# A four-layer graph network on one core: softmax passes with their weights in PSUM, sums placed by register and one wide addition, and query rows kept in fp32

## The reference

```
x += (segment_sum(h[src]) / (deg + eps)) @ W0.T + b0                        # sum
x += relu(mean over edges of relu([h[src], h[dst]] @ W_edge.T) @ Wn.T + bn)  # mlp
x += GAT(elu(GAT(h)))                                                        # gat, twice
x += attention(h) + h @ Wskip + bskip                                        # dot
```

## Time and profile before

| what | us |
| --- | --- |
| median of 3 runs | 5275.26 (5270.87 to 5277.76) |
| profiled execution | 5274.91 |
| its span | 5273.2 |
| busy PE, PE weight loads | 3318.3 (63%), 2774.7 (53%) |
| busy DVE | 2957.9 (56%) |
| busy ACT | 1684.9 (32%) |
| busy POOL | 3467.1 (66%) |

### The profile page before, as it was taken

One profiled execution on the slowest core, in us unless ns is written; L12 is line 12 of the kernel. 1 busy time (PEld: TensorE's weight loads), 2 busy tenths in 40 slices (PEclk: granted clock), 3 DMA queues, 4 the chain that ended last, 5 costly groups with the idle time before them and its releaser, 6 DMA issues. The chain is left out here.

```text
span 5273.2 us, 118399 instructions
## 1 busy us (share of the span) xinstructions
PE 3318.3 (63%) x30932; PEld 2774.7 (53%) x30933; DVE 2957.9 (56%) x8646; ACT 1684.9 (32%) x5942; POOL 3467.1 (66%) x3551
## 2 busy tenths in 40 slices
PE   1555555667777775666666646666666466666664
PEld 0444444456666563555555535555555355555554
DVE  3222222432222225777777767777777867777777
ACT  2222222332222225444444444444444411111111
POOL 1777777457777772777777537777775076666663
PEclk9666666666666667666666656666666767777776
DMA  4333333233333332444334224433442244444442
GB/s 123 105 106 107 104 104 104 70 100 104 106 106 104 104 87 72 111 109 115 110 109 112 81 73 112 112 109 109 113 110 76 69 144 137 135 139 136 140 135 82
DMA packets 331653, 564.80 MB, mean 107 GB/s; under 512 B 79101, under 2 KB 149773, under 8 KB 331438
## 3 DMA queue, kind: packets, MB, share of 16 engines
q0 software_dynamic: 124288, 289.37, 20.6%
q1 hardware_dynamic: 207170, 273.48, 16.7%
HBM read 490.38 MB, written 72.84 MB: 107 GB/s over the span
## 5 line engine op out<-in xcount | busy, mean ns | idle before, releaser
L1003 POOL DMA_INDIRECT GT<-table,srcI x3520 | 3452.8, 981 | 1687.3 <-issue 1044.2
L1316 PE MATMUL psA<-V,O 128*128 128x144 f32 (+1 forms) x4224 | 970.3, 414 | 45.3 <-DVE acc L1427 40.1
L1316 PEld LDWEIGHTS psA<-V,O 128*128 128x128 f32 x4224 | 901.6, 305 | 108.5 <-DVE acc L1427 75.3
L1427 DVE TENSOR_TENSOR acc<-acc,psA 128x144 f32 (+1 forms) x2112 | 624.7, 296 | 274.3 <-DVE acc L1427 7.6
L1044 DVE TENSOR_TENSOR acc<-acc,psA 128x1032 f32 (+1 forms) x176 | 214.7, 1220 | 685.9 <-PE psA L1123 673.0
L1168 DVE TENSOR_TENSOR prod<-psD,GT 128x1024 f32<-128x1024 f32 x88 | 107.7, 1224 | 679.5 <-DMA GT<-table,srcI 679.5
L1307 PE MATMUL psS<-newM,Ot 128*128 128x16 bf16 (+1 forms) x6336 | 213.2, 175 | 432.9 <-DVE newM L1394 432.9
L1035 PE MATMUL psA<-zerob 1*128 1x258 bf16 (+1 forms) x704 | 179.0, 405 | 484.8 <-issue 453.4
L1307 PEld LDWEIGHTS psS<-newM,Ot 128*128 128x128 bf16 x6336 | 189.6, 102 | 488.5 <-DVE newM L1394 488.5
L1250 ACT COPY nodeM<-newM 128x16 f32 x1408 | 307.8, 219 | 348.0 <-ACT nodeM L1250 226.3
L1181 PE MATMUL psD<-nodeQ,Ot 128*128 x2112 | 283.9, 264 | 130.8 <-DVE prod L1168 125.3
(11 more groups left out here) (217 smaller groups left out, 4965.8 us busy)
## 6 DMA issues: line engine op xcount, KB each, us to landing
Ob<-onehots SPq DMA_DIRECT2D x352, 256.0 KB
Ot<-onehots_turned SPq DMA_DIRECT2D x352, 256.0 KB
GT<-table,srcI POOLq DMA_INDIRECT x3520
onehots<-Ob SPq DMA_DIRECT2D x88, 256.0 KB
onehots_turned<-Ot SPq DMA_DIRECT2D x88, 256.0 KB
first<-first_dram SPq DMA_DIRECT2D x176, 64.0 KB
first_dram<-GT SPq DMA_DIRECT2D x18, 384.0 KB, 5.2
table<-GT SPq DMA_DIRECT2D x40, 144.0 KB, 1.9
```

What stands on the lines that cost most here:

```text
L1003: eng.indirect_dma_start(out=GT[:, p.k, j, 0:table.shape[1]], out_offset=None, in_=table, in_offset=bass.IndirectOffsetOnAxis(ap=srcI[:, p ...
L1316: ins = eng.matmul(psA[:, j, 0:VW], O[:, p.q, j, :], V[:, p.q, j, 0:VW], start=True, stop=True)
L1427: eng.tensor_tensor(a, a, psA[:, j, 0:VW], ALU.add).then_inc(added.sem, 1)
```

## The change

1. Softmax passes, weights: `act_weight` takes the exponential twice, first into PSUM (`factors`, in the fourth bank of `psA`) and then into `V` as before. `dve_values` multiplies by `factors` and so has one input in SBUF and one in PSUM.
2. Softmax passes, sums: the eight tiles of a group are summed into nine places of `psA` by block, three places in each of three banks, where a register gives the offset (`blk_off`, a new table made at the start by six DVE operations). Several tiles of one block accumulate in one place. `act_empty` on ACT writes zeros into the nine places first, once the addition of the group before is done. `dve_add` scales and then adds all nine places to nine consecutive blocks at once; it loads one block number instead of eight.
3. Order: PE does `pe_sums` of group p-2 right behind `pe_maxima` of group p. DVE's `dve_segmax` stands behind the addition. The logits of the target nodes go to the edges two turns ahead in gat too, and `act_stage` three.
4. Query rows (dot) and the target part in mlp: `nodeQ` is kept in fp32; ACT casts `Ot` to fp32 (`turn_32`), and PE does eight fp32 matmuls instead of 24 bf16 ones. The splitting into parts goes from `sum_to_mlp` and `gat_to_dot`. SP's load of `Ot` waits for the cast (`turned32`) instead of the matmuls, in dot beside `maxedge`.

The core of the diff:

```diff
+    PLACES, STRIDE, BANK = 9, 170, 512
...
-        nodeQ = sb("nodeQ", [P, NB, 3, D], BF16)
+        nodeQ = sb("nodeQ", [P, NB, D])
...
+        Ot32 = sb("Ot32", [P, 2, G, P])
...
-                            part_rest(eng, n, n.R[:, :, D:2 * D], kept)
-                            part_2(eng, n, D, nodeQ)
...
-                            eng.copy(n.R, n.ps).then_inc(kept.sem, 1)
-                            part_0(eng, n, n.R[:, :, D:2 * D], nodeQ, kept)
-                            part_1(eng, n, D, nodeQ)
+                            eng.copy(n.R[:, :, 0:D], n.ps[:, :, 0:D]).then_inc(kept.sem, 1)
+                            eng.copy(n.at(nodeQ), n.ps[:, :, D:2 * D]).then_inc(noted_rows.sem, 1)
...
-                            eng.scalar_tensor_tensor(out=n.Y2, in0=n.ps[:, :, 0:D], scalar=Q_SCALE, in1=bias_row(6),
+                            eng.scalar_tensor_tensor(out=n.at(nodeQ), in0=n.ps[:, :, 0:D], scalar=Q_SCALE, in1=bias_row(6),
...
+        def turn_32(eng, p):
+
+            eng.wait_ge(*ring_hotT[p.k](p.i))
+            eng.wait_ge(*toedge(p.g - 2))
+            eng.copy(Ot32[:, p.q, :, :], Ot[:, p.k, :, :]).then_inc(turned32.sem, 1)
+
+        def rows_to_edges(eng, p, b):
+
+            eng.wait_ge(*turned32(p.g))
+            eng.wait_ge(*prodded(p.g - 1))
+            for j in range(G):
+                ins = eng.matmul(psD[:, j, :], Ot32[:, p.q, j, :], at_block(nodeQ, b[j], D), start=True, stop=True)
+            ins.then_inc(toedge.sem, 1)
+
...
+            factors = flatA[:, 3 * BANK:3 * BANK + HG].rearrange("p (g h) -> p g h", g=G)
+            places = flatA[:, 0:3 * BANK].rearrange("p (m e) -> p m e", e=BANK)[:, :, 0:3 * STRIDE]\
+                .rearrange("p m (n w) -> p m n w", w=STRIDE)[:, :, :, 0:VW]
...
+            def act_empty(eng, p):
+
+                eng.wait_ge(*added(p.g - 1))
+                apart(eng)
+                eng.copy(places, consts[:, 0:1, :].unsqueeze(1).to_broadcast([P, 3, 3, VW])).then_inc(emptied.sem, 1)
+
             def act_weight(eng, p):
+
                 eng.wait_ge(*bound(p.g))
+                eng.wait_ge(*values(p.g - 1))
+                eng.activation(factors, by_head(below[:, p.q, 0:HG]), ACT.Exp).then_inc(factor.sem, 1)
                 eng.wait_ge(*sums(p.g - 2))
                 v = V[:, p.q, :, 0:VW].rearrange("p g (h c) -> p g h c", h=h)
                 eng.activation(v[:, :, :, C:C + 1], by_head(below[:, p.q, 0:HG]).unsqueeze(3), ACT.Exp).then_inc(weight.sem, 1)
...
+            def pe_places(eng, p):
+                return loaded(eng, "places", blk_off, p.g, G, 2 * BANK + STRIDE)
+
+            def pe_sums(eng, p, off):
                 eng.wait_ge(*values(p.g))
+                eng.wait_ge(*weight(p.g))
                 eng.wait_ge(*onehot32(p.g))
+                eng.wait_ge(*emptied(p.g))
+                apart(eng)
                 for j in range(G):
-                    if j % 2 == 0:
-                        eng.wait_ge(*added(p.g - 1, j + 1))
-                    ins = eng.matmul(psA[:, j, 0:VW], O[:, p.q, j, :], V[:, p.q, j, 0:VW], start=True, stop=True)
+                    ins = eng.matmul(flatA[:, bass.ds(off[j], VW)], O[:, p.q, j, :], V[:, p.q, j, 0:VW], start=False,
+                                     stop=j == G - 1, skip_group_check=True)
                 ins.then_inc(sums.sem, 1)
...
             def dve_values(eng, p):
-                eng.wait_ge(*weight(p.g))
+                eng.wait_ge(*factor(p.g))
+                eng.wait_ge(*sums(p.g - 2))
                 v = V[:, p.q, :, 0:VW].rearrange("p g (h c) -> p g h c", h=h)
-                eng.tensor_tensor(v[:, :, :, 0:C], heads(GT[:, p.k, :, f0:f0 + D], h),
-                                  v[:, :, :, C:C + 1].to_broadcast([P, G, h, C]), ALU.mult).then_inc(values.sem, 1)
-
-            def dve_scale(eng, p):
-
-                b = loaded(eng, "blocks", blk, p.g, G, NB - 1)
+                eng.tensor_tensor(v[:, :, :, 0:C], heads(GT[:, p.k, :, f0:f0 + D], h), wide(factors, C), ALU.mult)\
+                   .then_inc(values.sem, 1)
+
+            def dve_add(eng, p):
+
+                b = loaded(eng, "block", blk, p.g, 1, NB - 1, G)
                 a = at_block(acc, b[0], VW).rearrange("p (h c) -> p h c", h=h)
                 eng.wait_ge(*rescale(p.g))
                 eng.wait_ge(*added(p.g - 1))
                 eng.tensor_tensor(a, a, wide(resc[:, p.q, 0:h], C + 1), ALU.mult).then_inc(scaled.sem, 1)
-                return b
-
-            def dve_add(eng, p, b):
-
                 eng.wait_ge(*sums(p.g))
                 eng.wait_ge(*scaled(p.g))
-                for j in range(G):
-                    a = at_block(acc, b[j], VW)
-                    if j:
-                        eng.wait_ge(*added(p.g, j - 1))
-                    eng.tensor_tensor(a, a, psA[:, j, 0:VW], ALU.add).then_inc(added.sem, 1)
+                to = acc[:, bass.ds(b[0], PLACES), 0:VW].rearrange("p (m n) w -> p m n w", n=3)
+                eng.tensor_tensor(to, to, places, ALU.add).then_inc(added.sem, 1)
...
+                        if not gat and p.has(2):
+                            turn_32(eng, p.plus(2))
+                        if gat and p.has(3):
+                            act_stage(eng, p.plus(3))
+                        if p.has(1):
+                            act_flags(eng, p.plus(1))
                         if p.has(0):
                             act_rescale(eng, p)
-                        if gat and p.has(2):
-                            act_stage(eng, p.plus(2))
-                        if p.has(1):
-                            act_flags(eng, p.plus(1))
+                        if p.has(-1):
+                            act_empty(eng, p.plus(-1))
                         if p.has(0):
                             act_weight(eng, p)
                             if gat:
                                 act_note(eng, p)
                             act_onehot32(eng, p)
-                    sweep(eng, NG, turn, early=RING)
+                    sweep(eng, NG, turn, early=RING, late=1)
                 @block.tensor
                 def _(eng):
                     def turn(p):
+                        if p.has(-2):
+                            off = pe_places(eng, p.plus(-2))
                         if p.has(0):
                             pe_maxima(eng, p)
-                        if gat and p.has(1):
-                            pe_toedge(eng, p.plus(1))
+                        if p.has(-2):
+                            pe_sums(eng, p.plus(-2), off)
                         if p.has(1):
                             pe_logitT(eng, p.plus(1))
                         if p.has(0):
                             pe_maxedge(eng, p)
                         if p.has(1):
                             pe_segT(eng, p.plus(1))
-                        if not gat and p.has(2):
+                        if p.has(2):
                             pe_toedge(eng, p.plus(2))
-                        if p.has(-1):
-                            pe_sums(eng, p.plus(-1))
-                    sweep(eng, NG, turn, early=2, late=1)
+                    sweep(eng, NG, turn, early=2, late=2)
...
-                            b = dve_scale(eng, p.plus(-2))
+                            dve_add(eng, p.plus(-2))
                         if p.has(1):
                             dve_segmax(eng, p.plus(1))
-                        if p.has(-2):
-                            dve_add(eng, p.plus(-2), b)
                         if p.has(0):
```

79 lines of the change are left out of this document (34 added, 45 removed).

## The result

The changed kernel takes 5177.84 us (median of 4 runs, 5173.40 to 5181.22), the kernel before 5275.75 (4 runs, 5270.87 to 5277.76): a ratio of 0.9815, 95% interval 0.9802 to 0.9827. Forecast were 5171 and 5100 to 5235. The profiled execution took 5178.65, its span is 5176.9, 96.3 us less than before.

The account below looks back on a forecast made before the run. POOL's gathers were taken to bound the gat passes, a cycle through DVE and PE the dot pass. 5274.9 - 110 (gat) - 10 (sum_to_mlp) - 13.4 (gat_to_dot) + 30 (dot) = 5171.5, say 5171 us, range 5100 to 5235.

Parts of the forecast that it names:

- case A: Whole kernel: the terms come out as summed, 5171 us, own range 5140 to 5205; chance 0.50.
- the remainder of contention: Gat passes: short DVE operations with two SBUF inputs still hold POOL 0.05 us a turn (bounds 0 and 0.25).
- The whole difference is this one gather: Gat turn: a 1.62 us gather beside DVE's multiplication explains 10.66 against mlp's 9.98; PSUM weights save 110 us over both passes.
- Dot pass: Dot: the cycle closes through PE at 11.77 us a turn, +30 us for the pass (bounds -51 and +82).
- The 3.84 from product to new maxima: Dot turn: first term of the cycle, 3.84 us from DVE's product to the end of the maxima chain.
- fp32 rows: Dot turn: eight fp32 matmuls replace 24 bf16 ones, 3.6 us (bounds 3.2 and 3.8) instead of 3.21.
- sum_to_mlp: Node phase limited by ACT: two copies of 0.40 us each, 0.6 less a unit, 10 us taken (bounds 5 and 12).
- gat_to_dot: Node phase limited by DVE: two operations of 0.33 us each go, 0.67 x 20 = 13.4 us saved.
- B: Dot turn closes sooner, 10.9 to 11.3 us, -14 to -49 instead of +30: 5092 to 5127 us; chance 0.18.
- C: Gat passes: POOL's long gather stays, the 110 us are gone, 5281 us; chance 0.09.
- D: Gat turn ends at 10.2 to 10.5 us by ACT or PE's cycle: 63 instead of 110, 5218 us; chance 0.16.
- E: Gat passes: zeroing in front of ACT's exponential delays DVE's multiplication; with dot at its upper bound 5376 us, slower; chance 0.07.

Follow-up runs that it names:

- g1_psum_weights: The kernel before with only the gat weights moved to PSUM: 5264.75 us against 5273.37, ratio 0.9982.
- g3_scan_first: The changed kernel with DVE's scan in front of the wide addition in the dot pass: 5016.04 us against 5273.23 for the kernel before, ratio 0.9515.
- g7_bf16_rows: The changed kernel without its fourth part, query rows in three bf16 parts again: 5204.55 us against 5273.37 for the kernel before, ratio 0.9871.
- h9_three_passes: The changed kernel plus SBUF weights (gat 1), 1.05 us more ACT work (gat 2), query rows before the transpose (dot): 6842.33 us against the kernel before's 6945.72.
- f3_scan_first: The changed kernel with DVE's scan before the wide addition in the dot pass, on a slower chip: ratio 0.9893 to the kernel before.
- e2_sbuf_weights: The changed kernel with DVE's multiplication reading its weights from SBUF again, on a slower chip: ratio 0.9947 to the kernel before.
- g2_sbuf_weights: The changed kernel with DVE's multiplication reading its weights from SBUF again, asked again, on a slower chip: ratio 1.0013 to the kernel before.

## Why the prediction was right

- **The sign and the size.** Forecast -103, measured -96 in the profiled executions, as case A: POOL's pace in gat, PE's cycle in dot. Of the signs named ahead, the gat passes missed theirs by a little (890.0 and 889.7 us for 880 to 888).
- **Gat passes.** The end point was right (10.03 a turn forecast; 890.0 + 1.2 over 88 is 10.13), the remainder of contention was under-sized: 0.05 taken, 0.14 measured (12.0 us over 0.944 a gather, in 88 turns), inside the bounds of 0 and 0.25. That is some 8 us a pass, the whole miss. The reason was half right. "The whole difference is this one gather" is true of POOL's rows, but POOL was not what set the turn: DVE was called the second limit by its work (8.0 us), and its round with the waits was 10.72, above POOL's 10.66. `g1_psum_weights` shows that the edit that is credited with the 110 us brings nothing by itself. The sum came out because it goes by the end point, where no other engine's turn was to be above 10.03, and DVE, still at 10.73 with the weights alone moved, got there only with the other edits of the softmax passes.
- **The rule on interference** (the Trainium skill, SBUF — State Buffer, "Who interferes with whom"): the traces agree in its main statement. One input moved to PSUM, and the gather beside the 1.21 us multiplication takes 0.94 in two kernels. Its other half shows too: L1407 of the changed kernel, with two inputs in SBUF, holds a gather for 0.1 to 0.2 us, so "nearly nothing" in the prediction should have read 0.14 a turn. The two scans in front of it, also with both inputs in SBUF, hold none, and no run here shows why.
- **Dot pass.** Right term by term (table above), and shown by taking the scan out of it: `g3_scan_first`. One term was in part luck. The 3.84 from product to new maxima was read from one turn; over 86 turns of the kernel before the mean is 4.41, with which the sum gives +77 us. In the kernel before DVE stands 0.47 us a turn inside this step, in front of L1359, which reads PE's maxima (24.7 + 11.9 us over 78 turns), in the changed one not at all. The prediction does not say that this wait would go. The load of one register was 0.71 from start to start, 0.54 of it idle. The floor of 600 ns in the Trainium skill (DMA: Bandwidth & Descriptors, "Latency and other measured facts") would put the term at 0.6 or more; the term is above that, its idle part below. With such a floor the lowest turn of the prediction would be 11.17 and not 11.57, since its lower bound has the query rows at 3.2 too.
- **fp32 rows.** The block itself was sized rightly (3.6 forecast, 3.71). What the sum left out is that other matmuls change with it: by `g7_bf16_rows` the pass would be 6.6 us longer, not 44 shorter, with the shorter block.
- **sum_to_mlp** (-17 for -10). ACT's two copies that read PSUM start 0.27 apart, not the 0.40 that each lasts, so the unit fell from 3.66 to 2.82 and not by 0.6. Timeline, beside the earlier trace rows:

```profile
1040.35 0.38 ACT L669 COPY GT<-psS 128x256 f32<-128x256 f32 x1
...
1040.62 0.39 ACT L670 COPY nodeQ<-psS 128x256 f32<-128x256 f32 x1
...
1040.88 0.40 ACT L568 COPY Ob<-psA 128x256 f32<-128x256 f32 x1
```

- **gat_to_dot** (-8.3 for -13.4). In the earlier trace rows L570 stood between two operations of which the second waits for the first. With it gone they are 0.45 apart, not 0.33: it had been cover for a latency. The unit fell by 0.56 (5.25 to 4.69), not by 0.67, and the rest came at the ends of the phase:

```profile
4026.66 0.41 DVE L928 TENSOR_TENSOR O<-psT,bias 128x256 f32<-128x256 f32 x1
...
4027.11 0.42 DVE L930 TENSOR_TENSOR X<-X,O 128x256 f32<-128x256 f32 x1
```

- **Rivals.** B (a dot turn under 11.3), C (the long gather stays) and D (10.2 to 10.5 in gat) did not come. Of E, the wait is there but not the cost. In the gat turn shown above zeroing ends at 2559.85, 0.55 us after DVE's last operation on `below` (2559.04, 0.26 long), and the exponential starts only then. It should cost nothing, since DVE waits 1.7 us a turn for rows behind it; the run that was to test this (`h9_three_passes`) fell on another kind of chip.

## What to carry to other kernels

When a stage's turn comes close to one engine's sum, measure the other engines' rounds too, waits and register loads included, before crediting the whole gap to one edit: here two limits lay 0.06 us apart, and the edit that freed one showed nothing alone. A stage's gain is read from its start to the start of the next: the last gather alone came 5 and 7 us sooner, and the stage was as long as before. When work on an engine shrinks, ask what now stands directly in front of the instruction that feeds the next engine: here an addition of 1.4 us in front of a scan of 0.4 cost 142 us, and exchanging the two beat both kernels. A shorter block on PE is no gain when the block behind it then runs at the lower clock more often.

## What the runs showed of the hardware

**Chips differ, and in a way that hides a change.** On four chips the kernel before took 1.30 to 1.32 times as long. The timeline of `f3_scan_first` in a gat turn there:

```profile
3211.43 0.75 PE L1290 MATMUL psD<-stageD,Ot 128*128 128x16 bf16 x11
...
3212.55 0.94 POOL L1000 DMA_INDIRECT GT<-table,srcI  x1 [0.30 <-issue]
3213.44 0.17 PE L1290 MATMUL psD<-stageD,Ot 128*128 128x16 bf16 x1 [1.26 <-issue]
...
3215.56 0.17 PE L1290 MATMUL psD<-stageD,Ot 128*128 128x16 bf16 x1 [1.96 <-issue]
```

In the middle of a block of 24 matmuls that wait for nothing PE issues one at a time, up to 2.1 us apart, while POOL issues the gathers of its group at its usual pace; one turn earlier DVE stood too:

```profile
3202.87 0.29 DVE L1418 TENSOR_TENSOR below<-lg,psS 128x128 f32<-128x128 f32 x1 [6.65 <-remote]
```

It went on 1.8 us after POOL's eighth gather had ended (3201.08), and over 78 turns of this pass it is 1.7 us on average. POOL then waits 5.2 us itself, for DVE to release the next rows. So from about the middle of a group's gathers until a little behind the last, DVE and ACT stand and PE issues single matmuls, and POOL stands after that; a gat turn takes 15 us and not 10.1. What is shared there the profile doesn't name, and it was not tested. On such a chip the change as a whole may be worth little or nothing (`e2_sbuf_weights` and `g2_sbuf_weights`, which are all of it but one read, are at 0.9947 and 1.0013), while the order of the dot pass is still worth 1 to 2%.

**The same matmuls, two clocks.** In the dot pass of the changed kernel the 16 matmuls of the sums (L1334) take 2.05 us in one turn and 3.83 in another; the windows view has the granted clock at 1.00 in one of the first kind and at 0.50 in one of the second, the two levels of 2.4 and 1.2 GHz. Of 88 turns 12 take 3.7 us or more; with the query rows in bf16 it is 76 of 88, and the mean of a matmul is 417 ns and not 328. What the rest of a turn does to the clock is part of the price of an edit on PE.
